# Three steps of the first batch's normalisations, and one copy, from VectorE to ScalarE in the second scan of a two-block network

## What is computed

```python
x = x + L0_conv(_ln_c(x))          # state-space block
t = _to_tokens(x)
t = t + L0_ffn(_ln_t(t))           # 8 experts, top 2
x = _from_tokens(t, x)
x = x + L1_conv(_ln_c(x), A)       # decaying sum along 128 channels
t = _to_tokens(x)
t = t + L1_ffn(_ln_t(t))           # 16 experts, top 2

# inside L0_conv, for every token t, 256 inner channels d, 16 states n:
dA = exp(dt_t[..., None] * A)
h  = dA * h + (dt_t * x_t)[..., None] * B_t[:, None, :]
y  = einsum('bdn,bn->bd', h, C_t)
# then y + xc*D, times silu(z), out_proj, clamp, layernorm, clamp, added to x

# L0_ffn(v): xf = layernorm(v)*g + b
logits = xf @ gate_w; probs = softmax(logits); top-2 combine weights
out = sum_e combine[:, e] * (gelu(xf @ w1[e] + b1[e]) @ w2[e] + b2[e])
return v + out                     # v itself is a layernorm of t: two in a row
```

## Time and profile before

| | us |
|---|---|
| median of three timed runs | 209.47 (208.74 to 210.15) |
| the profiled execution | 210.71 |
| its span, first to last instruction | 208.6 |
| around the span | 2.1 |

### The profile page before, as it was taken

How to read it: one execution, slowest core, us unless ns; L and a number is a source line. 1 busy time by engine, 2 the same in 40 slices (tenths; PEclk the granted TensorE clock), 3 DMA queues, 4 the chain that set the end, 5 groups by cost and what they waited for, 6 DMA issues and landing times. The chain is left out here.

```text
span 208.6 us, 3721 instructions
## 1 busy us (share of the span) xinstructions
PE 183.1 (88%) x1202; PEld 152.8 (73%) x1202; DVE 136.0 (65%) x319; ACT 119.9 (57%) x274; POOL 104.4 (50%) x136
## 2 busy tenths in 40 slices
PE   6899868996696459699998999999998999999993
PEld 5677744642262235287997989999997999999992
DVE  2575999998999999961374755654258483434433
ACT  2717998999730049142666657767565555455540
POOL 5510044779779846395356426544465444444500
PEclk9999999999999988789999999999999999999999
DMA  5950399996550000000000000000000000000000
GB/s 158 328 164 0 82 357 349 325 321 187 201 204 2 0 0 0 0 0 0 3 2 0 3 0 2 3 0 0 3 2 0 3 0 2 3 25 5 0 0 25
DMA packets 7233, 14.38 MB, mean 69 GB/s; under 512 B 512, under 2 KB 3112, under 8 KB 6960
## 3 DMA queue, kind: packets, MB, share of 16 engines
q1 hardware_dynamic: 7216, 14.17, 21.3%
HBM read 13.88 MB, written 0.29 MB: 68 GB/s over the span
## 5 line engine op out<-in xcount | busy, mean ns | idle before, releaser
L343 POOL TENSOR_TENSOR hc<-hs,cb 128x1024 f32<-128x1024 f32 x16 | 37.7, 2356 | 29.8 <-DVE hs L724 16.8
L848 DVE SCALAR_TENSOR_TENSOR acc<-dbx_ps,comb,acc 128x128 f32<-128x128 f32 x96 | 29.0, 345 | 33.4 <-PE dbx_ps L1123 33.0
L1099 PE MATMUL bc_ps<-x_hi,w_hi 128*128 128x256 f32 x128 | 42.5, 332 | 0.0
L566 ACT ACTIVATE hid<-bc_ps,par 128x256 f32<-128x256 f32 x64 | 26.8, 471 | 25.0 <-PE bc_ps L1101 24.9
L357 POOL TENSOR_TENSOR w_lo<-w1b,w_hi 128x256 fp32r<-128x256 f32 x32 | 23.5, 735 | 27.5 <-ACT w_hi L558 27.2
L724 DVE TENSOR_TENSOR_SCAN hs<-da,dbx_ps 128x1024 f32<-128x1024 f32 x16 | 36.5, 2279 | 0.1
L1101 PE MATMUL bc_ps<-x_hi,w_lo 128*128 128x256 f32 x128 | 36.4, 285 | 0.0
L1100 PE MATMUL bc_ps<-x_lo,w_hi 128*128 128x256 f32 x128 | 36.3, 283 | 0.0
L1123 PE MATMUL dbx_ps<-w2b,hid 128*128 128x128 f32 (+1 forms) x256 | 33.9, 277 | 0.8 <-DVE acc L848 0.8
L1123 PE MATMUL dbx_ps<-w2a,hid 128*128 128x128 f32 x256 | 34.3, 277 | 0.3 <-ACT hid L566 0.2
L357 POOL TENSOR_TENSOR w_lo<-w1a,w_hi 128x256 fp32r<-128x256 f32 x32 | 23.1, 732 | 20.0 <-ACT w_hi L558 20.0
(11 more groups left out here) (171 smaller groups left out, 234.4 us busy)
## 6 DMA issues: line engine op xcount, KB each, us to landing
w1a<-w_in SPq DMA_DIRECT2D x2, 1024.0 KB, 8.2
cb<-c_rows SPq DMA_DIRECT2D x2, 1024.0 KB, 5.7
w1b<-w_in SPq DMA_DIRECT2D x2, 1024.0 KB, 12.8
cb<-c_rows SPq DMA_DIRECT2D x2, 768.0 KB, 5.7
cb<-taps_in SPq DMA_DIRECT2D x1, 512.0 KB, 5.6
cb<-c_rows SPq DMA_DIRECT2D x2, 256.0 KB, 3.4
par<-packed_in SPq DMA_DIRECT2D x1, 473.0 KB, 3.9
x_cm<-x_in SPq DMA_DIRECT2D x2, 128.0 KB, 2.2
```

Source lines behind the costliest of these rows:

```text
L343: nc.gpsimd.tensor_tensor(hc[p][:], hs[p][:], cb[:, k].rearrange("p i (o t) -> p i o t", o=1).to_broadcast([128, PAIR, DC, T]), ALU.mult). ...
L566: ins = nc.scalar.activation(hid[p][:, c, :], h_ps[p][:, T * c:T * (c + 1)], ACT.Gelu, bias=par[:, bass.ds(u * UC + at, 1)])
L848: nc.vector.scalar_tensor_tensor(acc[k][:, t, :], o_ps[:, w // span % RING, 128 * t:128 * (t + 1)], comb[layer][b][:, t, bass.ds(u, 1)], a ...
L1099: nc.tensor.matmul(h_ps[p][:, T * c:T * (c + 1)], w1_hi[w][:, at], x_hi[b][:], start=True, stop=False)
```

## The change

It is made of four edits.

1. ScalarE takes three of DVE's steps for the first batch: the norm in `skip_norm` (now `skip_scale`, ahead of the states of pair 2), the norm in `inner_norm` (pair 3) and the scaling in `inner_scale` (pair 3). As an activation it is x*scale + bias, so POOL makes `shift` = -mean*rstd by two more tiny operations after root 3 and after root 4. DVE keeps the clamp, the sums and the statistics, and waits for ACT's results.
2. In the second scan ACT makes decay factors three pairs ahead: four pairs at pair 0, then pair k + 3 at pair k.
3. The copy of the transposed combine weights (`gates_tc`) of the first batch is ACT's.
4. `zsum` in `softmax_e`, and the remainder `left` in `gates` (all four calls), lie in PSUM instead of SBUF.

```diff
+        m_zsum = m_ps[:, T + 32:T + 32 + TT]
+        m_left = [m_ps[:, T + 64:T + 64 + TT * (n + 8)].rearrange("p (t e) -> p t e", t=TT) for n in EXPERTS]
-        before_states = {1: ["gate_out", "out_proj"], 3: ["inner_norm", "root_5"], 4: ["logits"], 5: ["softmax_e"],
+        before_states = {1: ["gate_out", "out_proj"], 2: ["skip_scale"], 3: ["inner_norm", "root_5"], 4: ["logits"], 5: ["softmax_e"],
@@ POOL
+            def shifted(k):
+                link(nc.gpsimd.tensor_tensor(shift[:], mv[0][:, :, 0], rstd[0][:], ALU.mult))
+                nc.gpsimd.tensor_scalar(shift[:], shift[:], -1.0, None, ALU.mult).then_inc(s["shift" + k], 1)
+                    if b == 0 and step in ("root_3", "root_4"):
+                        pool.wait_ge(s["rstd" + which], 1)
+                        shifted(which)
@@ ACT
             def pair_in(b, k):
-                decays(b, k, (k + NP * b) % AHEAD)
+                for j in (range(AHEAD) if b and k == 0 else (k + AHEAD - 1,) if b else (k,)):
+                    if j < NP:
+                        decays(b, j, (j + NP * b) % AHEAD)
+            def skip_scale(layer, b):
+                act.wait_ge(s["shift3"], 1)
+                for t in range(TT):
+                    ins = nc.scalar.activation(m_norm[:, t, :], norm_a[b][:, t, :], ACT.Identity, scale=rstd[b][:, t:t + 1],
+                                               bias=shift[:, t:t + 1])
+                ins.then_inc(s["skip_scaled"], 1)
...
+                act.wait_ge(s["shift4"], 1)
+                for t in range(TT):
+                    ins = nc.scalar.activation(m_tok[:, t, :], t_tok[b][:, t, :], ACT.Identity, scale=rstd[b][:, t:t + 1],
+                                               bias=shift[:, t:t + 1])
+                ins.then_inc(s["inner_done"], 1)
...
+                act.wait_ge(s["rstd5"], 1)
+                act.wait_ge(s["sum_done"], 1)
+                for t in range(TT):
+                    ins = nc.scalar.activation(xg_tok[b][:, t, :], m_tok[:, t, :], ACT.Identity, scale=rstd_b[b][:, t:t + 1])
+                ins.then_inc(s["xn_tok"], 1)
...
+                act.wait_ge(s["comb_ps"], 1)
+                nc.scalar.activation(combT[b][:], m_ps[0:EXPERTS[0], 0:T], ACT.Copy).then_inc(s["combT_ready"], 1)
@@ DVE
+                if b:
+                    link(normalise(TT, m_norm, norm_a[b], mv[b], rstd[b], "rstd3", b))
+                else:
+                    dve.wait_ge(s["skip_scaled"], 1)
...
+                if (layer, b) == (0, 0):
+                    dve.wait_ge(s["inner_done"], 1)
+                    nc.vector.tensor_tensor(t_tok[b][:], t_tok[b][:], m_tok, ALU.add).then_inc(s["sum_done"], 1)
+                    return
...
-                link(nc.vector.reciprocal(zsum[b][:], zsum[b][:]))
+                link(nc.vector.reciprocal(m_zsum, zsum[b][:]))
...
-                pr, rest_p = prob[layer][b], left[layer][b]
+                pr, rest_p = prob[layer][b], m_left[layer]
```

More of the change, by code:

```diff
@@ L85 @@
 b_ready dbx_done da_done h_done hc_done y_done
-yz_ready o_ps var3 rstd3 var4 rstd4 rstd5 xn_tok xn_ps x_full x_hi_ready xsplit logit_ps z_sub z_tanh comb_ready
+yz_ready o_ps var3 shift3 skip_scaled inner_done sum_done shift4 rstd3 var4 rstd4 rstd5 xn_tok xn_ps x_full x_hi_ready xsplit logit_ps z_sub z_tanh comb_ready
 comb_ps combT_ready b2_ps
@@ L150, in bass_metaformer @@
         rstd_b = per_batch("rstd_b", [128, TT])
+        shift = sb("shift", [128, TT])
         norm_a = per_batch("norm_a", [128, TT, C])
@@ L163, in bass_metaformer @@
         prob = [[sb(f"prob_{l}_{b}", [128, TT, EXPERTS[l] + 8]) for b in range(NB)] for l in range(2)]
-        left = [[sb(f"left_{l}_{b}", [128, TT, EXPERTS[l] + 8]) for b in range(NB)] for l in range(2)]
         top2 = per_batch("top2", [128, TT, 8])
@@ L527, in pair_in, with inner_norm, inner_scale, gates_tc @@
             def pair_in(b, k):
-                decays(b, k, (k + NP * b) % AHEAD)
+                for j in (range(AHEAD) if b and k == 0 else (k + AHEAD - 1,) if b else (k,)):
+                    if j < NP:
+                        decays(b, j, (j + NP * b) % AHEAD)
             def stage(u):
                 high_part(0, u, u)
+            def skip_scale(layer, b):
[4 more added lines that the diff above has]
+                ins.then_inc(s["skip_scaled"], 1)
+            def inner_norm(layer, b):
+                if b:
[5 more added lines that the diff above has]
+                ins.then_inc(s["inner_done"], 1)
+            def inner_scale(layer, b):
+                if layer or b:
+                    return
+                act.wait_ge(s["rstd5"], 1)
[3 more added lines that the diff above has]
+                ins.then_inc(s["xn_tok"], 1)
+            def gates_tc(layer, b):
+                if b:
+                    return
+                act.wait_ge(s["comb_ps"], 1)
+                nc.scalar.activation(combT[b][:], m_ps[0:EXPERTS[0], 0:T], ACT.Copy).then_inc(s["combT_ready"], 1)
             def exp_logits(layer, b):
@@ L589, in _ @@
                     "bc_copy": bc_copy, "silu1": silu1, "stage": stage,
-                    "pair_in": pair_in, "exp_logits": exp_logits, "expert_in": expert_in,
+                    "pair_in": pair_in, "exp_logits": exp_logits, "skip_scale": skip_scale, "inner_norm": inner_norm, "inner_scale": inner_scale,
+                    "gates_tc": gates_tc, "expert_in": expert_in,
                     "softmax": softmax, "experts": experts}
@@ L748, in skip_norm @@
                 dve.wait_ge(s["xtok_ready"], b + 1)
-                link(normalise(TT, m_norm, norm_a[b], mv[b], rstd[b], "rstd3", b))
+                if b:
+                    link(normalise(TT, m_norm, norm_a[b], mv[b], rstd[b], "rstd3", b))
+                else:
+                    dve.wait_ge(s["skip_scaled"], 1)
                 link(clamp(m_norm, m_norm))
@@ L756, in inner_norm @@
             def inner_norm(layer, b):
-                link(normalise(TT, m_tok, t_tok[b], mv[b], rstd[b], "rstd4", b))
+                if b:
+                    link(normalise(TT, m_tok, t_tok[b], mv[b], rstd[b], "rstd4", b))
             def inner_scale(layer, b):
+                if (layer, b) == (0, 0):
+                    dve.wait_ge(s["inner_done"], 1)
+                    nc.vector.tensor_tensor(t_tok[b][:], t_tok[b][:], m_tok, ALU.add).then_inc(s["sum_done"], 1)
+                    return
                 if layer == 0:
@@ L801, in softmax_e @@
                 link(nc.vector.tensor_reduce(out=zsum[b][:], in_=ex[:], op=ALU.add, axis=AX.X))
[L802 removed]
+                link(nc.vector.reciprocal(m_zsum, zsum[b][:]))
                 link(nc.vector.tensor_tensor(prob[layer][b][:, :, 0:n], ex[:],
[L804 removed]
+                                             m_zsum.rearrange("p (t o) -> p t o", o=1).to_broadcast([128, TT, n]), ALU.mult))
             def gates(layer, b):
                 n = EXPERTS[layer]
[L809 removed]
+                pr, rest_p = prob[layer][b], m_left[layer]
                 for t in range(TT):
@@ L827, in gates_tc @@
             def gates_tc(layer, b):
+                if b == 0:
+                    return
                 dve.wait_ge(s["comb_ps"], b + 1)
```

1 line of the change is left out of this document (removed).

## The result

The changed kernel takes 214.31 us in the median of six executions (211.69 to 214.72), the kernel before beside it on the same chip 209.81 (208.74 to 210.43). The ratio is 1.0181, with a 95% interval of 1.0142 to 1.022: slower by 3.8 us in the ratio of the comparison, by 4.5 in the medians. The forecast was 210.7, with 208.3 to 212.2 as its range. It was wrong.

The account below looks back on a forecast made before the run. The prediction took the time as PE's start, released by scan b1k5, plus some 116 us of stream. A start 1.2 us later, between +1.6 and +0.6 by clock, on 209.47 gave 210.7 us, range 208.3 to 212.2.

Parts of the forecast that it names:

- What bounds the kernel: Whole kernel: time is a start plus some 116 us of PE's expert stream; scan b1k5 releases PE, later DVE work is off the path.
- DVE's relief ahead of scan b1k5: Second scan: the relief goes into waiting for POOL and ACT, and scan b1k5 starts 0.23 us later.
- The row behind the transpose: ACT before `output(0)`: copy, table load and first Gelu stand in a row, starting `output(0)` 1.8 us late at 91.35.
- Rival (b): At `output(0)`: PE really follows scan b1k6 and the Gelu comes in time; 207.9, or 204.9 with all relief; chance 0.13.
- Rival (c): ACT behind the transpose: a gap behind the table load makes the start 2.1 to 3.1 us late; 211.6 to 212.6; chance 0.14.
- PSUM operands: DVE's `prob` and `comb` fall to 0.17 us each, 0.55 and 1.49 less; the latter buys only slack at `output(0)`.
- The clock: PE around add b1k5: sum is +1.6 us if the clock falls, +0.6 if it stays up; taken as +1.2.
- Slower by over 1%: Whole kernel: a median over 211.6 us, from a first Gelu later than forecast or a gap behind the table load; chance 0.18.
- The Gelu's part: At `output(0)`: the first Gelu holds it, late by 0 to 2.1 us; median 209.2 to 211.5; chance 0.64.

Follow-up runs that it names:

- busy gap: Changed kernel plus six empty identity products on PE ahead of `output(0)`, filling its idle; 211.48 us, ratio 1.0071 to the kernel before.
- longer gap: Changed kernel plus one more table load, of another set, behind ACT's copy of the combine weights; 216.08 us, ratio 1.0284 to the kernel before.
- traced long execution: The changed kernel run again unchanged, for a trace of one of its slower executions; 214.36 us.
- early load: Changed kernel with ACT loading the Gelu table ahead of its wait for the transpose; 210.06 us, ratio 0.9996 to the kernel before.

## Why the prediction was wrong

**What bounds the kernel: right.** The time is a start and a stream; the last column shows it over seventeen traces. What the prediction did not say is that the stream has two lengths. And that DVE's work behind scan b1k5 is not on the path holds for the trace it read, with the low clock ahead of the start. At full clock `output(0)` waits for scan b1k6, 0.54 us in the kernel with edits 1 and 2.

**DVE's relief ahead of scan b1k5 is spent on waiting: right.** Low parts forecast for 68.1, measured 68.21; `hc` b1k2 69.47 and 69.58; `inner_norm` 73.42 and 73.66; scaling 75.06 and 75.18; `x_full` 77.2 and 77.29; `mx` 78.75 and 78.55; scan b1k5 80.8 and 80.61. Edits 1 and 2 alone gave a ratio of 1.0005, and with DVE's copy moving the high parts and decay factors out of the way gave the relief back. The pair with two pointer operands took 0.84 us, the pair with one 0.62, for the 0.87 and 0.64 assumed.

**The row behind the transpose: right, but not what it is compared with.** Load forecast for 89.15, measured at 88.81; Gelu 90.45 and 90.11; `output(0)` 91.35 and 91.05. The busy gap gives this step by itself: ratio 1.0071, 1.5 to 1.8 us. The forecast of +1.2 was the middle of +1.6, with the clock low ahead of both starts, and +0.6, with it low in the kernel before alone. The profiled pair is of the first kind and has +1.4 in the distance, +1.3 in the span. The second compares a full clock with a low one: at full clock in both it is 29.71 to 30.14 against the 28.3 estimated, +1.4 to +1.8. So the step costs about 1.5 us at either clock. The idle ahead of add b1k5, forecast to shrink to 1.6 us, was 1.93. Rival (b) has fallen for this change, as the first `output` waits for ACT; but its wait for scan b1k6 is real, as said above. Rival (c), a gap behind the load, has fallen: the gap is 0.02 us, in the longer gap's two loads in a row too.

**PSUM operands: the durations right, the worth too small.** `prob` and `comb` came down to the 0.17 us forecast in both kernels. Alone the edit gave 1.6 us in the ratio and 2.0 from the start's distance, where 0.54 is what the scan gained. The prediction held that the stall on `comb` buys only slack. At full clock it buys some 0.7 us at scan b1k6, by the estimate above; the rest of the 2.0 in the distance is the clock in the trace of the kernel before. The stalls end with POOL's operation beside them: `comb` at 85.31 and POOL's `hc` at 85.27, with edits 1 and 2 alone at 85.65 and 85.62. The Trainium skill gives the reason, page "SBUF — State Buffer", section "Who interferes with whom": a DVE instruction with two SBUF inputs contends with a GpSimd instruction that reads SBUF. The traces agree: 1.66 us with both in SBUF and 0.17 with one in PSUM.

**The clock: the failed step.** It says: "Even if it falls, it has risen again by 91.3, and `output(0)` and the bias product run 0.2 us faster than before." This looked at one low stretch, that of 86 to 90 us in the one trace at hand, and asked whether it would stay. In the profiled execution that is just what happened (0.58 from 86 to 90, and 0.99 behind 90), so the trace landed within about 0.3 us of every number above. But the change makes a second idle of PE, 1.4 to 2 us, only some 3 us behind the first of 1.9 (4.3 us in the profiled execution, where the clock was low between the two). The prediction priced it as idle time and not as what idle time does to the clock behind it, though its own rows had an idle of 2.06 us next to a stretch at 0.57. What failed is thus the term for the clock behind `output(0)`, put at 0.2 us gained, where the traced long execution lost 3.2 us. In nine of fifteen executions the time is longer by about that loss (one of the nine was traced, and there the clock fell at the start of the stream, where every microsecond counts, and cost 3.2 us). The sum should have read +1.5 in the short executions and +4.7 in the long ones: 209.47 + 1.5 = 211.0, where the six short ones have a median of 211.03, and 214.2, where the nine long ones have 214.36.

The evidence that the idle is the cause, by its size: 0.24 us of it (early load), 0.56 (busy gap): no long execution in eighteen. 1.4 to 2 us: nine in fifteen. About 3 us (edit 3 alone, longer gap): all twelve at 215 us or more. That PE's idle decides it, and not ACT's lateness, is shown by the busy gap, where ACT was as late and the long executions were gone. The 12 at 3 us also start later by the longer idle itself; that the clock fell in them is read from one trace of each kernel.

**What stays open.** Why one execution of the same kernel falls in one group and the next in the other is not shown. The traces are alike but for where the clock went down ahead of 90 us: about 70 to 77 and then again from 90.6 in the long one; 70 to 76 and 86 to 90, or 72 to 82 (two traces), or 72 to 75 and 79 to 82, in the short ones. A low stretch shortly before goes with none behind `output(0)`, and the rows show what else is different: in the last three of these short ones PE, slowed before, comes to the addition of b1k5 with no idle ahead of it, or 0.52 us, where the long one has 1.92. Their idle of 1.95 or 1.96 us ahead of `output(0)` stands alone, and the clock stays up behind it. So in the traces it took both idles; but one long trace is not enough for a rule, and the kernel with edit 3 alone has one low stretch at 85 to 88 and another at 91 to 98. The longer gap lost more clock (123.1) than the change (122.0) with the same stretch at 70 to 77. Nor does the clock averaged over an execution tell the group: 0.968 in one of 212.25 us, 0.976 in one of 213.47. It depends on where the clock is low. That the other eight long executions lost their time where the traced one did is inferred from their times, and from the busy gap and the early load, where none was long.

**The chances.** Slower by over 1% had 0.18, all of it from a later Gelu. The Gelu's part came as forecast; what carried the time out of the range is the clock behind it, which was not among the rivals.

## What to carry to other kernels

A wait on an engine holds up what stands behind it in its queue, and a table load is a part of what stands there: before a small operation is moved to ScalarE, look whether the next activation behind it needs another table, and load that table ahead of the wait. An idle of TensorE is to be priced twice, by its length and by the clock of the work behind it; a gap of 1.4 to 2 us at the head of a dense stream cost up to 3.2 us more here, and filling it with empty products took that back. Work that hides behind a slow stretch is not off the path: price both kernels at the same clock. When one trace carries a forecast that rests on a clock, take the number as one draw: the same kernel gave spans of 207.7 to 212.9 us.
